# Graph attention on one core: behind each group of scores the projection runs before the transposes of x

## The chip, the cores and the metric

The kernel runs on one core of a Trainium2 chip. The metric is the device time of one execution in microseconds; the runs shown are given by their median. Five engines work side by side and wait for each other only through semaphores: TensorE (PE, with its weight loads as PEld), VectorE (DVE), ScalarE (ACT), GpSimd (POOL) and SyncE (SP), which issues the transfers.

## The reference, cut to what matters

```
x [32, 256, 384], adj [32, 256, 256]; 12 heads of 32 columns
q, k, v = x @ Wq + bq, x @ Wk + bk, x @ Wv + bv          (split into heads)
scores  = q @ k.T / sqrt(32) + beta * adj                 (-9e15 where adj <= 0)
probs   = softmax(scores)
out     = layernorm(x + probs @ v)                        (eps 1e-5)
```

## The kernel before, in words

A block is one of the B = 32 graphs. It has T = 2 tiles of 128 rows, C = 3 chunks of 128 input columns, G = 3 groups of J = 4 heads, so H = 12 heads. While block n goes through its heads h = 0 to 11, projections of block n + 1, transposes of block n + 2 and the values of block n - 2 are worked on in between.

TensorE's work outside the scores is cut into jobs, named by kind, part and block. Each writes one of four PSUM banks (`j_bank`), by its place in the ring modulo 4, and waits until the job four places earlier has been taken out of its bank (`wait_taken`).

- X(c, n): two transposes of chunk c of x (`turn_x`, L396). ACT copies the result to `xt_high` (L538), and DVE then subtracts that from the bank to make `xt_low` (L616). DVE's part waits for ACT's.
- K(g, n), Q(g, n), V(t, n): projections of nine matmuls (`project`, L387 for K and Q, L384 for V), taken by ACT alone (L534, L536).
- O(g, n): probabilities times values (`values`, L416), taken by ACT (L544). G(g, n): the result turned back (`turn_heads`, L424), taken by DVE (L623).
- T(h, n): four transposes of one head's probabilities (`turn`, L433), taken by ACT (L530) in the blocks up to the last. Only heads 10 and 11 go this way; the first ten are transposed by DVE in 32 x 32 pieces (`turn_blocks`, L635), and shuffled by DMA.

After the jobs of heads 0, 4 and 8 TensorE runs the sixteen score matmuls of the next group of four heads (`scores`, L463) into four `s_bank`s, each head in its own. Head 8 is followed by group 0 of block n + 1. Before them it waits until DVE has taken every maximum of the group before (`max_ready`).

DVE takes two maxima per head from `s_bank` (`maxima`, L600), which also write `neg_scores`. ACT follows with the two exponentials (`exps`, L518). ACT's order in head h is `exps` of head h + 2 and then the jobs of h in the order of the table. DVE's order in heads 1 and 5 is the maxima of heads h + 3 and h + 4 and then X; in head 9 X stands between the two (heads 12 and 13 there are heads 0 and 1 of the next block). Behind X come G, the maxima of head h + 4 at h = 2, 6 and 10, and in block n's head 10 one `turn_blocks`, then, in head 11, the maxima of head 15 (head 3 of the next block).

The order of everything is written out by hand in `jobs_of`: TensorE's program, ACT's and DVE's are all made from that one table, and so is the ring of banks. The change touches the table of the middle blocks, n = 1 to 30 (L81 to L95). Block n + 2 exists up to n = 29, so 29 blocks have X jobs by this table.

Of the kernel before, what the change touches and what calls it, by code (L numbers as in the profile page):

```python
# [34 lines left out]
def graph_attention_program(nc, x, adj, wq, bq, wk, bk, wv, bv, beta, out):  # L35
# [22 lines left out]
    def by_blocks(n, h):  # L58
        return h < block_heads(n)
# [5 lines left out]
    def jobs_of(n, h):  # L65
        if n == 0:

            jobs = {
                0: (("K", 2, 0),),
                1: (("K", 0, 1),),  # L70
                2: (("Q", 0, 1),),
                3: (("K", 1, 1),),
                4: (("V", 0, 0),),
                5: (("Q", 1, 1),),
                6: (("V", 1, 0), ("Q", 2, 1)),
                7: (("V", 0, 1),),
                9: (("X", 0, 2), ("K", 2, 1)),
                10: (("X", 1, 2),),
                11: (("X", 2, 2), ("V", 1, 1)),
            }  # L80
        elif n < B - 1:  # L81
            jobs = {
                0: (("O", 0, n - 2),),
                1: (("X", 0, n + 2), ("K", 0, n + 1)),
                2: (("G", 0, n - 2), ("Q", 0, n + 1)),
                3: (("K", 1, n + 1),),
                4: (("O", 1, n - 2),),
                5: (("X", 1, n + 2), ("Q", 1, n + 1)),
                6: (("G", 1, n - 2), ("Q", 2, n + 1)),
                7: (("V", 0, n + 1),),  # L90
                8: (("O", 2, n - 2),),
                9: (("X", 2, n + 2), ("K", 2, n + 1)),
                10: (("G", 2, n - 2),),
                11: (("V", 1, n + 1),),
            }  # L95
        else:
            jobs = {
                0: (("O", 0, n - 2),),
                1: (("O", 1, n - 2),),
                2: (("G", 0, n - 2), ("O", 2, n - 2)),  # L100
                3: (("G", 1, n - 2),),
                4: (("G", 2, n - 2),),
                5: (("O", 0, n),),
                7: (("G", 0, n), ("O", 0, n - 1)),
                8: (("O", 1, n - 1),),
                9: (("G", 0, n - 1), ("O", 2, n - 1), ("G", 1, n - 1), ("O", 1, n)),
                10: (("G", 2, n - 1), ("G", 1, n)),
            }
        turn = () if by_blocks(n, h) else (("T", h, n),)
        return turn + tuple(job for job in jobs.get(h, ()) if 0 <= job[2] < B)  # L110
# [4 lines left out]
    second_jobs = (("K", 1, 0),) + tuple(("X", c, 1) for c in range(C))  # L115
    last_jobs = (("O", 2, B - 1), ("G", 2, B - 1))
    ring = [*first_jobs, *second_jobs, *(job for n in range(B) for h in range(H) for job in jobs_of(n, h)), *last_jobs]
    place = {job: r for r, job in enumerate(ring)}

# [33 lines left out]
    with ctx:  # L153
# [216 lines left out]
        def _(pe):  # L370
# [124 lines left out]
            for n in range(B):  # L495
                for h in range(H):
                    jobs = jobs_of(n, h)
                    if not by_blocks(n, h):
                        run(jobs[0])
                        jobs = jobs[1:]  # L500
                    for job in jobs:
                        run(job)
                    if h % J == 0:
                        if h < H - J:
                            scores(n, h // J + 1)
                        elif n + 1 < B:
                            scores(n + 1, 0)
# [4 lines left out]
        def _(act):  # L512
# [58 lines left out]
            for n in range(B):  # L571
                for h in range(H):
                    s = H * n + h
                    if s + 2 < B * H:
                        exps(s + 2)
                    for job in jobs_of(n, h):
                        take(job)
# [388 lines left out]
```

## Time and profile before

| | us |
|---|---|
| median of 3 runs (lowest, highest) | 622.64 (622.37, 623.55) |
| profiled execution | 621.97 |
| its span | 620.1 |
| PE busy | 601.8 |
| DVE busy | 582.7 |
| ACT busy | 574.8 |
| POOL busy | 492.6 |

The span is the time from the first to the last instruction on the core; 1.87 us of the execution lie around it. Busy times are unions of the instructions' spans. Matmuls overlap in the array, so the distance from one group's first weight load to the next group's tells more of TensorE than the busy time does.

### The profile page before, as it was taken

The numbers are of one execution on the slowest core, as the hardware profiler recorded it, in microseconds if no ns is written. First come the engines' busy times: TensorE is split into PE (matmuls) and PEld (weight loads), VectorE is DVE, ScalarE is ACT, GpSimd is POOL, SyncE is SP. The second block draws the span as 40 slices with busy tenths as digits, with TensorE's granted clock in tenths as the row PEclk, the third lists the DMA queues.
The fourth block names the chain that finished last, engine by engine and source line by source line (L and its number), as shares of the span: only waits on it lengthen the run. The fifth ranks groups of instructions, "written<-read, shape, count | busy, mean of one in ns | idle before, by whom it ended". The sixth has DMA issues, their size and how long they took to land. (4 is left out here: it accounts for less than half of the span.)

```text
span 620.1 us, 20691 instructions
## 1 busy us (share of the span) xinstructions
PE 601.8 (97%) x6080; PEld 488.2 (79%) x6080; DVE 582.7 (94%) x2235; ACT 574.8 (93%) x2063; POOL 492.6 (79%) x669
## 2 busy tenths in 40 slices
PE   8999999999999999999999999999999999999991
PEld 7887878787888878787878788888878787878760
DVE  4989999999999999999999999999999999999786
ACT  4999999999999999999999999999999999999981
POOL 1334448988888888888898888898888889889793
PEclk9999999999999999999999999999999999999996
DMA  6258879988888988888998888898888898887832
GB/s 202 80 120 193 180 169 220 203 193 203 200 201 198 236 177 202 201 203 195 220 199 196 203 201 199 202 222 185 203 202 200 197 227 187 201 201 176 198 92 101
DMA packets 56190, 117.61 MB, mean 190 GB/s; under 512 B 10512, under 2 KB 12304, under 8 KB 56080
## 3 DMA queue, kind: packets, MB, share of 16 engines
q1 hardware_dynamic: 54992, 116.10, 80.6%
q8 instruction: 50, 0.82, 0.6%
q14 instruction: 60, 0.49, 0.3%
q10 hardware_dynamic: 1088, 0.20, 0.2%
HBM read 22.94 MB, written 12.58 MB: 57 GB/s over the span
## 5 line engine op out<-in xcount | busy, mean ns | idle before, releaser
L518 ACT ACTIVATE probs<-neg_scores,neg_max 128x256 f32<-128x256 f32 x768 | 382.5, 504 | 1.8 <-DVE neg_max L600 1.3
L600 DVE CUSTOM_DVE_ANT_0 neg_scores<-s_bank,bias_sb 128x256 f32<-128x256 f32 x768 | 280.1, 414 | 16.3 <-PE s_bank L463 15.1
L635 DVE STREAM_TRANSPOSE blocks<-probs 128x512 f32<-128x512 f32 x308 | 196.8, 685 | 0.3 <-ACT probs L518 0.3
L518 ACT ACTIVATION_READ_ACCUMULATOR probs<-neg_scores,neg_max 128x1 f32 x768 | 150.9, 197 | 0.0
L463 PE MATMUL s_bank<-qk 32*128 32x256 f32 x1536 | 110.0, 400 | 1.0 <-ACT qk L534 0.6
L387 PE MATMUL j_bank<-xt_high,w_high 128*128 128x256 f32 x567 | 110.1, 302 | 0.3 <-ACT qk L534 0.3
L534 ACT ACTIVATE qk<-j_bank,qk_bias 128x256 f32<-128x256 f32 x192 | 89.9, 469 | 21.0 <-PE j_bank L387 17.6
L463 PEld LDWEIGHTS s_bank<-qk 32*128 32x128 f32 x1536 | 69.5, 184 | 41.0 <-ACT qk L534 13.1
L898 POOL TENSOR_SCALAR att<-att,rstd,shift 128x384 f32<-128x384 f32 x58 | 95.7, 1656 | 6.3 <-POOL shift L895 6.3
L416 PE MATMUL j_bank<-shuffled,v_sb 128*32 128x256 f32 x1232 | 98.1, 385 | 0.2 <-ACT blocks L530 0.2
L387 PE MATMUL j_bank<-xt_high,w_low 128*128 128x256 f32 x567 | 97.0, 279 | 0.0
L387 PE MATMUL j_bank<-xt_low,w_high 128*128 128x256 f32 x567 | 96.9, 279 | 0.0
L862 POOL TENSOR_TENSOR att<-att,x_sb 128x768 f32<-128x768 f32 x30 | 55.5, 1850 | 39.2 <-DVE att L623 38.4
L387 PEld LDWEIGHTS j_bank<-xt_high,w_high 128*128 128x128 f32 x567 | 79.4, 189 | 2.3 <-issue 1.8
L387 PEld LDWEIGHTS j_bank<-xt_low,w_high 128*128 128x128 f32 x567 | 79.7, 188 | 0.0
L387 PEld LDWEIGHTS j_bank<-xt_high,w_low 128*128 128x128 f32 x567 | 79.6, 188 | 0.0
L843 POOL TENSOR_SCALAR bias_sb<-adj_sb 128x512 f32<-128x512 f32 x30 | 59.9, 1998 | 22.4 <-DMA adj_sb<-in_adj_dram 16.7
L846 POOL TENSOR_SCALAR adj_sb<-adj_sb,beta_col 128x512 f32<-128x512 f32 x31 | 62.1, 2004 | 13.3 <-DVE bias_sb L648 10.2
L856 POOL TENSOR_TENSOR x_sb<-x_sb,bv_row 128x768 f32<-128x768 f32 x32 | 59.1, 1848 | 8.2 <-DMA bv_row<-in_L_gnn_bv_dram 7.9
L416 PEld LDWEIGHTS j_bank<-shuffled,v_sb 128*32 128x32 f32 x1232 | 37.2, 109 | 35.2 <-issue 15.1
L600 DVE DVE_READ_ACCUMULATOR2_ANT neg_max<- 128x1 f32 x768 | 63.9, 83 | 0.0
L888 POOL TENSOR_SCALAR nt_b<-var_eps,rstd 128x1 f32<-128x1 f32 x174 | 58.3, 347 | 6.5 <-POOL rstd L881 6.2
(81 smaller groups left out, 918.4 us busy)
## 6 DMA issues: line engine op xcount, KB each, us to landing
shuffled<-blocks SPq DMA_DIRECT2D x480, 160.0 KB, 4.2
x_sb<-in_x_dram SPq DMA_DIRECT2D x32, 384.0 KB, 6.1
out_dram<-att SPq DMA_DIRECT2D x30, 384.0 KB, 4.0
adj_sb<-in_adj_dram SPq DMA_DIRECT2D x32, 256.0 KB, 6.2
shuffled<-blocks SPq DMA_DIRECT2D x16, 128.0 KB, 2.5
blocks<-in_L_gnn_Wq_dram SPq DMA_DIRECT2D x1, 576.0 KB, 5.7
blocks<-in_L_gnn_Wk_dram SPq DMA_DIRECT2D x1, 576.0 KB, 8.0
blocks<-in_L_gnn_Wv_dram SPq DMA_DIRECT2D x1, 576.0 KB, 5.0
```

What stands on the lines that cost most here:

```text
L387: mm = pe.matmul(b[:, 0:N], wp[:, q, c, a * P:(a + 1) * P], xp[:, n % 2, c, :], start=(m == 0), stop=(m == 3 * C - 1))
L416: mm = pe.matmul(b[HD * j:HD * (j + 1), 0:N], v_sb[:, n % 4, k, h * HD:(h + 1) * HD], probs_k, start=(k == 0), stop=(k == T - 1))
L463: mm = pe.matmul(s_bank[j][:, t * N:(t + 1) * N], qk[rows, n % 2, 0, g, t * P:(t + 1) * P], qk[rows, n % 2, 1, g, :], start=True, stop=True)
L518: nc.scalar.activation(probs[:, (T * s + t) % (T * NX), :], neg_scores[:, (T * s + t) % (T * NH), :], ACT.Exp, bias=neg_max[:, n % 2, t, h ...
L534: ins = nc.scalar.activation(qk[:, n % 2, q, a, :], b[:, 0:N], ACT.Identity, bias=qk_bias[:, q, a:a + 1])
L600: nc.vector.tensor_tensor_reduce(neg_scores[:, (T * s + t) % (T * NH), :], s_bank[h % J][:, t * N:(t + 1) * N], bias_sb[:, n % 2, t, :], - ...
L635: nc.vector.transpose(blocks[:, n % 2, :, h, :, :].rearrange("p k t q -> p t k q"), probs[:, slot:slot + T, :].rearrange("p t (k q) -> p t ...
L843: nc.gpsimd.tensor_scalar(key_order(bias_sb[:, n % 2, :, :]), by_keys(adj_sb[:, :, :]), 0.0, MASKED, ALU.is_le, ALU.mult).then_inc(not_edg ...
L846: nc.gpsimd.tensor_scalar(adj_sb[:, :, :], adj_sb[:, :, :], 0.0, beta_col[:, 0:1], ALU.max, ALU.mult).then_inc(adj_beta_ready, 1)
L856: nc.gpsimd.tensor_tensor(x_sb[:, n % XB, :, :], x_sb[:, n % XB, :, :], bv_row[:, :].unsqueeze(1).to_broadcast([P, T, D]), ALU.add).then_i ...
L888: b_at[t] = link(nc.gpsimd.tensor_scalar(nt_b[:, t:t + 1], var_eps[:, t:t + 1], rstd[:, t:t + 1], rstd[:, t:t + 1], ALU.mult, ALU.mult))
L898: nc.gpsimd.tensor_scalar(att[:, n % 3, t, :], att[:, n % 3, t, :], rstd[:, t:t + 1], shift[:, t:t + 1], ALU.mult, ALU.subtract).then_inc( ...
```

## The change

In the middle blocks the projection that stands in the same head as an X job is put ahead of it, at heads 1, 5 and 9. No job is added or taken away.

```diff
         elif n < B - 1:
             jobs = {
                 0: (("O", 0, n - 2),),
-                1: (("X", 0, n + 2), ("K", 0, n + 1)),
+                1: (("K", 0, n + 1), ("X", 0, n + 2)),
                 2: (("G", 0, n - 2), ("Q", 0, n + 1)),
                 3: (("K", 1, n + 1),),
                 4: (("O", 1, n - 2),),
-                5: (("X", 1, n + 2), ("Q", 1, n + 1)),
+                5: (("Q", 1, n + 1), ("X", 1, n + 2)),
                 6: (("G", 1, n - 2), ("Q", 2, n + 1)),
                 7: (("V", 0, n + 1),),
                 8: (("O", 2, n - 2),),
-                9: (("X", 2, n + 2), ("K", 2, n + 1)),
+                9: (("K", 2, n + 1), ("X", 2, n + 2)),
                 10: (("G", 2, n - 2),),
                 11: (("V", 1, n + 1),),
             }
```

## Rows read from the trace of the kernel before

**Rows 1.** Page, part 1: busy time, share of the span, instructions of each engine.
```profile
PE 601.8 (97%) x6080; PEld 488.2 (79%) x6080; DVE 582.7 (94%) x2235; ACT 574.8 (93%) x2063; POOL 492.6 (79%) x669
```
**Rows 2.** Windows: busy time of each engine, PE clock, DMA share, GB/s.
```profile
core 0: us, PE busy (x) PEld busy (x) DVE busy (x) ACT busy (x) POOL busy (x), PEclk, DMA share, GB/s
41.50:580.00 538.50, 538.09 (x5493) 437.57 (x5495) 523.47 (x2022) 518.19 (x1883) 452.13 (x601) 1.00 0.88 200
250.26:268.61 18.35, 18.35 (x193) 14.91 (x190) 18.14 (x71) 17.64 (x66) 16.31 (x23) 1.00 0.87 201
```
**Rows 3.** Waits: who waited for whom; us in total, times, longest.
```profile
ACT qk L534 <- PE j_bank L387: 17.6, 44, 0.5
DVE neg_scores L600 <- PE s_bank L463: 15.1, 32, 1.6
```
**Rows 4.** Timeline of weight loads, one block: start, us, ..., [idle before <- releaser].
```profile
250.26 0.74 PEld L463 LDWEIGHTS s_bank<-qk 32*128 32x128 f32 x16 [0.41 <-ACT v_sb L536]
251.33 0.20 PEld L396 LDWEIGHTS j_bank<-ident,x_sb 128*128 128x128 f32 x2 [0.33 <-ACT heads_t L544]
251.50 0.42 PEld L387 LDWEIGHTS j_bank<-xt_high,w_high 128*128 128x128 f32 x3
...
252.57 0.46 PEld L433 LDWEIGHTS j_bank<-ident,probs 128*128 128x128 f32 x4
253.00 0.25 PEld L424 LDWEIGHTS j_bank<-ident,heads_t 128*128 128x128 f32 x2
253.22 0.47 PEld L433 LDWEIGHTS j_bank<-ident,probs 128*128 128x128 f32 x4
253.66 0.48 PEld L384 LDWEIGHTS j_bank<-w_high,xt_high 128*128 128x128 f32 x3
...
256.43 0.74 PEld L463 LDWEIGHTS s_bank<-qk 32*128 32x128 f32 x16 [0.41 <-ACT probs_t L530]
...
262.28 0.74 PEld L463 LDWEIGHTS s_bank<-qk 32*128 32x128 f32 x16 [0.41 <-ACT qk L534]
...
268.60 0.74 PEld L463 LDWEIGHTS s_bank<-qk 32*128 32x128 f32 x16 [0.41 <-ACT v_sb L536]
```
**Rows 5.** Timeline of weight loads in block 30, which has no X job.
```profile
575.27 0.41 PEld L387 LDWEIGHTS j_bank<-xt_high,w_high 128*128 128x128 f32 x3 [0.33 <-issue]
...
576.33 0.24 PEld L424 LDWEIGHTS j_bank<-ident,heads_t 128*128 128x128 f32 x2
576.54 0.42 PEld L387 LDWEIGHTS j_bank<-xt_high,w_high 128*128 128x128 f32 x3
```
**Rows 6.** Timeline of ACT around head 9 of the same block as Rows 4.
```profile
251.99 0.36 ACT L538 ACTIVATE xt_high<-j_bank 128x256 fp32r<-128x256 f32 x1
252.88 0.47 ACT L534 ACTIVATE qk<-j_bank,qk_bias 128x256 f32<-128x256 f32 x1 [0.52 <-PE j_bank L387]
253.25 0.50 ACT L518 ACTIVATE probs<-neg_scores,neg_max 128x256 f32<-128x256 f32 x1
```
**Rows 7.** Timeline of DVE from head 9 on, the same block.
```profile
252.39 0.42 DVE L616 TENSOR_TENSOR xt_low<-j_bank,xt_high 128x256 fp32r<-128x256 f32 x1
252.73 0.41 DVE L600 CUSTOM_DVE_ANT_0 neg_scores<-s_bank,bias_sb 128x256 f32<-128x256 f32 x1
...
253.53 0.42 DVE L623 TENSOR_TENSOR att<-j_bank,inv_sum 128x256 f32<-128x256 f32 x1
...
255.84 0.08 DVE L600 DVE_READ_ACCUMULATOR2_ANT neg_max<- 128x1 f32 x1
...
261.29 0.09 DVE L600 DVE_READ_ACCUMULATOR2_ANT neg_max<- 128x1 f32 x1
...
269.95 0.42 DVE L600 CUSTOM_DVE_ANT_0 neg_scores<-s_bank,bias_sb 128x256 f32<-128x256 f32 x1 [0.37 <-PE s_bank L463]
```
**Rows 8.** Timeline in block 0, where scores came right behind DVE's maxima.
```profile
24.62 0.08 DVE L600 DVE_READ_ACCUMULATOR2_ANT neg_max<- 128x1 f32 x1
...
24.82 0.77 PEld L463 LDWEIGHTS s_bank<-qk 32*128 32x128 f32 x16 [0.37 <-issue]
...
25.93 0.19 PEld L387 LDWEIGHTS j_bank<-xt_high,w_high 128*128 128x128 f32 x1 [0.33 <-issue]
```

## The prediction

> **What bounds the kernel now.** I read the page's first part, then the windows, the waits, and one block's timelines side by side. Part 1 shows TensorE busy for 97% of the span, DVE for 94% and ACT for 93% [rows 1], so TensorE leads but two others are close. The windows say it more sharply: over the 538.5 us of the middle TensorE is busy for 538.09 at a granted clock of 1.00, and in one block of 18.35 us it is busy throughout, DVE for 18.14 and ACT for 17.64 [rows 2]. TensorE sets the pace. DVE has 0.2 us of slack by that, a little more by its waits: its one regular wait is for the scores, 0.47 us a block (15.1 us in 32 times), and ACT's is for the projections, 17.6 us in 44 times [rows 3]. In the block that I follow, the scores start at 250.26, 256.43, 262.28 and 268.60 [rows 4]: legs of 6.17 (from group 0's scores in head 8 to the next), 5.85 and 6.32, together 18.34.
>
> What the reader should look at is how near DVE's release of the scores comes. The scores at 256.43 need all maxima of the group before, and the last of these ends at 255.84 + 0.08 = 255.92 [rows 7]. Those at 262.28 have theirs at 261.29 + 0.09 = 261.38. How long TensorE takes from such a release is seen in block 0: maximum over at 24.70, first weight load at 24.82, so 0.12 us [rows 8]. The first slack is thus 256.43 - 256.04 = 0.39 us, the second 262.28 - 261.50 = 0.78 us. A delay on DVE of more than 0.39 us between heads 9 and 0 stops TensorE.
>
> **The change part by part.** No instruction is added or removed. There are 3 places in each of 29 blocks (n = 1 to 29), 87 in all, and no DMA moves; SP's and POOL's programs are the same. All three engines' orders change, because all come from the table.
>
> *TensorE's own time.* Before, scores, X, K, next: X's loads start 1.07 after those of the scores, of which 0.33 is idle (the full-width load waits behind the row-packed scores), X takes 251.50 - 251.33 = 0.17 and K 252.57 - 251.50 = 1.07 [rows 4]. Block 30 shows K right behind the scores: the same 0.33 idle, and 576.33 - 575.27 = 1.06 [rows 5]. So K gains 0.01, and the idle stays. No row shows X behind K, but G is the same kind of job (two f32 transposes of 128x128): behind K and ahead of K it takes 576.54 - 576.33 = 0.21 [rows 5], between two T jobs 253.22 - 253.00 = 0.22 [rows 4]. X then costs 0.21, and the G or T behind it, which now follows a transpose and not a projection, 0.01 more. The sum at a place is -0.17 + 0.21 + 0.01 - 0.01 = +0.04. Its bounds: X behind K could be as cheap as now (0.17, which with K's gain makes -0.01) and as dear as 0.22, with 0.01 behind it (+0.05). I take 0.04, since G is nearest. Were that all, 87 x 0.04 = 3.5 us.
>
> The Trainium skill would have it otherwise (TensorE: Matmul & The Clock Gate, "Back-to-back issue gap"): it gives N/2.4 + 2.5 ns from one warm matmul to the next, 56 ns at N = 128. By it X behind K would cost 0.11 us and each place would gain 0.06. The trace has 0.11 per transpose wherever f32 transposes follow one another (T's four take 253.66 - 253.22 = 0.44 [rows 4]), twice the page's figure, so I keep the row's and put the page's result among the rivals.
>
> *ACT, in order.* Before, ACT takes X at 251.99 while K still runs, then idles 0.52 until K is released at 252.88 [rows 6]: X's copy is hidden in that gap. Now K comes first. K's result is there 0.17 + 0.01 earlier, at 252.70; ACT has been free since 251.99 and waits 0.71 for it. K's copy holds ACT for 0.37 (252.88 to 253.25), so X's copy starts at 253.07 and ends 0.36 later, at 253.43. Before, it ended at 252.35. Queued behind are the exponentials, which start some 0.1 us later than before; nobody waits for them that soon.
>
> *DVE, in order.* `xt_low` started 0.04 behind the end of ACT's copy (252.35 to 252.39 [rows 7]); now it starts at 253.47, **1.08 us later**. In head 9 the maxima of one head only stand ahead of it, so DVE stalls, and queued behind it are the maxima of the next head, G, two more heads' maxima and one block transpose. One pause behind it goes: the two maxima from 252.73 would be over at 253.42, G came at 253.53, so 0.11 was a wait for G. The last maximum of the group is then over at 255.92 + 1.08 - 0.11 = 256.89, and 0.12 later the scores load: 257.01 and not 256.43. **That is 0.58 us in this leg**, in which TensorE's own 0.04 is contained. Scores that had to wait fill an emptied array: 25.93 - 24.82 = 1.11 against 251.33 - 250.26 = 1.07, so 0.03 more [rows 4, 8]. Bounds for both together: 0.46 with no release time and no refilling, 0.71 with a further 0.1 us for handovers that the rows don't show.
>
> *Heads 1 and 5.* Both heads' maxima stand ahead of X there, 0.69 us more cover. `xt_low` can't start before the scores' start + 3.21 (253.47 - 250.26). DVE now arrives at about that moment, as it has run 0.97 us later since head 9; its stall is under 0.1 us. The maxima that release the scores of head 4 are over at 261.38 + 0.97 + 0.06 = 262.41, plus 0.12 is 262.53, and TensorE is there at 262.28 + 0.58 + 0.03 + 0.04 = 262.93. So TensorE leads these legs: +0.04 each. Back at head 8 the first maximum waits for the scores again (1.35 us behind their start: 268.60 to 269.95), and DVE arrives at that time within 0.1 us, so the lateness doesn't add up from block to block.
>
> *Banks.* T(11), four places behind K, needs K's copy (252.70 + 0.47 + 0.12 = 253.29) and is due at 253.26; that is nothing. The job four places behind X is now V(1) in head 11; it needs `xt_low`, over at 253.47 + 0.42, and the release of 0.12 makes 254.01. V stood at 253.66, with the place's own 0.04 at 253.70. It waits 0.31, and V and O lead to the scores 2.77 later (256.43 - 253.66), at 256.78. That is ahead of 257.01, so it lies beneath DVE's release; if that release were not there, this wait would cost 0.35 in its place.
>
> *Sum.* 0.58 + 0.03 + 2 x 0.04 = 0.69 us a block, a period of 19.04. Times 29 it is 20.0 us. On the profiled execution, 620.1 + 1.87 around it = 621.97, it gives 642.0; the median is 0.67 above that execution, so 642.7.
>
> **The rivals.**
> *Only TensorE's order counts.* If the maxima reach their release with DVE's stall inside the slack, 3.5 us remain: 626. For it: TensorE is the engine that is always busy, and the slack of 0.39 is real. Against it: the stall less the pause is 0.97, and the bank wait lies behind it.
> *The bank wait alone.* If the release is cheaper than I read it and V's wait decides, the leg costs 0.35, the block 0.43 and the whole 12.5 us: 635.
> *All three legs stall.* If handovers cost 0.2 more than the rows say in each leg, and the 0.4 us of slack at heads 1 and 5 is used up, the block costs 1.0 to 1.1: 621.97 + 29 x 1.05 + 0.67 = 653.
> *Not slower.* X behind K is fully overlapped: it costs 0.11, the place gains 0.06, 87 places gain 5.2 us, and the DVE stall is absorbed: 617. It decides once X behind K costs less than 0.18. For it speaks that the transposes' first load now runs beneath K's last matmul; against it, G in just that position takes 0.21. With X at 0.17 to 0.18 this case lands within 1 us of before.
> *The change doesn't do what it says.* The order is taken from the table by all engines, and the 29 blocks with X lie under it. I see no way for it to stay without effect, and give it nothing of its own.
>
> **How the numbers follow.** The forecast (638 to 648) has 0.62, the bank wait or a partly hidden stall (630 to 638) 0.15, TensorE's order alone (624 to 628) 0.08, all legs 0.09, not slower 0.06. A change of under 0.2% (1.2 us) can't be told from none here. The last case splits into 0.03 faster and 0.03 the same, all others are slower: 0.94. The range from 630 to 650 holds 0.8 of this. It takes in the bounds of the first leg, which give 638 (29 x 0.54) and 646 (29 x 0.79) on the median.
>
> **What would show it.** Right: in the windows a period near 19.0; in the waits a new line of the scores (L463) waiting for DVE's neg_max, once a block, about 0.5 us; ACT's wait for the projection at L534 up from 0.52 to about 0.7 in head 9; `xt_low` (L616) waiting for `xt_high` some 1.0 us in head 9 and hardly in heads 1 and 5; DVE's wait for the scores nearly gone; X's loads 0.21 apart from the next job's. Wrong: scores with no wait for DVE, then the time is 626 or less; waits at all three groups' scores, then it is 650 or more. The step that I trust least is the handover chain K, ACT, ACT, DVE, maxima, scores, since each link was read from one place.

## The result and the profile after

The changed kernel takes 642.79 us (median of 4 executions) against 622.50 before. The ratio is 1.0325, 95% interval 1.0311 to 1.0340: 3.3% slower. One of the four executions was disturbed (2480 us) and is left out of the ratio; the other three lie between 642.30 and 643.17, with a median of 642.41, which is 19.9 us above before. The forecast was 642.7, in a range of 630 to 650.

The profiled execution took 643.17 us, with a span of 641.4. Part 1 of its page, which answers to [rows 1], and two windows, which answer to [rows 2] (the middle, and one block from group 0's scores to the next group 0's):

```profile
PE 613.2 (96%) x6080; PEld 494.2 (77%) x6080; DVE 582.9 (91%) x2235; ACT 582.6 (91%) x2063; POOL 491.8 (77%) x669
```
```profile
41.50:580.00 538.50, 530.12 (x5300) 427.86 (x5299) 504.08 (x1948) 506.97 (x1816) 432.88 (x576) 1.00 0.83 193
259.15:278.24 19.09, 18.82 (x193) 15.15 (x189) 17.92 (x70) 17.94 (x65) 16.31 (x23) 1.00 0.78 195
```

The counts of instructions are those of before. TensorE, which had 0.4 us of idle time in these 538.5 us, now has 8.4, and the block went from 18.35 to 19.09 us. Busy time of DVE and ACT per block hardly moved (18.14 to 17.92, 17.64 to 17.94), so no engine does more; they wait more. The granted clock is 1.00 in both windows, so it isn't the clock.

The waits of the changed kernel, beside [rows 3]:

```profile
...
DVE xt_low L616 <- ACT xt_high L538: 40.2, 36, 6.1
PEld s_bank L463 <- ACT v_sb L536: 31.2, 57, 0.8
ACT qk L534 <- PE j_bank L387: 31.0, 61, 1.7
...
PE s_bank L463 <- DVE neg_max L600: 7.7, 31, 0.4
...
DVE neg_scores L600 <- PE s_bank L463: 5.8, 6, 1.4
...
PE j_bank L387 <- DVE w_low L744: 1.3, 1, 1.3
```

Two of these lines stood so before:

```profile
PEld s_bank L463 <- ACT v_sb L536: 11.9, 29, 0.4
...
DVE xt_low L616 <- ACT xt_high L538: 7.9, 5, 6.2
```

The line that grew most is DVE waiting for `xt_high`, from 7.9 us in 5 times to 40.2 in 36. The line that costs is a small one further down, and hardly there before (0.2 us, once): the scores waiting for DVE's maxima, once a block. It shows 7.7 us, 0.25 a time, and not 17 (29 x 0.58), for two reasons. The same wait of the scores is also on their weight loads, where it is put down to ACT: their idle time there went from 0.41 to 0.69 in the rows below, 0.28 more. And another 0.27 of the block has gone by already, in V(1)'s wait for its bank: the idle time of 0.24 at 262.87, where V(1) comes 0.71 behind T(11) and not 0.44. With TensorE's own 0.05 this makes the 0.60 by which the leg is longer. The last line is in the start and not in the blocks: a projection of block 0 waited 1.3 us for weights, which the change doesn't touch.

The timeline of weight loads in that block, which answers to [rows 4] (columns: start, us, what, [idle before <- releaser]):

```profile
259.15 0.74 PEld L463 LDWEIGHTS s_bank<-qk 32*128 32x128 f32 x16 [0.41 <-ACT v_sb L536]
260.23 0.42 PEld L387 LDWEIGHTS j_bank<-xt_high,w_high 128*128 128x128 f32 x3 [0.33 <-ACT heads_t L544]
...
261.30 0.24 PEld L396 LDWEIGHTS j_bank<-ident,x_sb 128*128 128x128 f32 x2
261.51 0.47 PEld L433 LDWEIGHTS j_bank<-ident,probs 128*128 128x128 f32 x4
261.94 0.25 PEld L424 LDWEIGHTS j_bank<-ident,heads_t 128*128 128x128 f32 x2
262.16 0.47 PEld L433 LDWEIGHTS j_bank<-ident,probs 128*128 128x128 f32 x4
262.87 0.47 PEld L384 LDWEIGHTS j_bank<-w_high,xt_high 128*128 128x128 f32 x3 [0.24 <-issue]
...
264.63 0.59 PEld L416 LDWEIGHTS j_bank<-shuffled,v_sb 128*32 128x32 f32 x16 [0.25 <-issue]
265.91 0.77 PEld L463 LDWEIGHTS s_bank<-qk 32*128 32x128 f32 x16 [0.69 <-ACT v_sb L536]
...
271.83 0.74 PEld L463 LDWEIGHTS s_bank<-qk 32*128 32x128 f32 x16 [0.41 <-ACT qk L534]
...
278.24 0.31 PEld L463 LDWEIGHTS s_bank<-qk 32*128 32x128 f32 x8 [0.41 <-ACT v_sb L536]
```

ACT and DVE beside it, answering to [rows 6] and [rows 7]:

```profile
261.60 0.47 ACT L534 ACTIVATE qk<-j_bank,qk_bias 128x256 f32<-128x256 f32 x1 [0.49 <-PE j_bank L387]
261.97 0.38 ACT L538 ACTIVATE xt_high<-j_bank 128x256 fp32r<-128x256 f32 x1
```
```profile
262.38 0.42 DVE L616 TENSOR_TENSOR xt_low<-j_bank,xt_high 128x256 fp32r<-128x256 f32 x1 [1.10 <-ACT xt_high L538]
...
263.40 0.42 DVE L623 TENSOR_TENSOR att<-j_bank,inv_sum 128x256 f32<-128x256 f32 x1
...
265.72 0.08 DVE L600 DVE_READ_ACCUMULATOR2_ANT neg_max<- 128x1 f32 x1
```

And TensorE's two transposes of X, before and changed; their ends are modelled:

```profile
251.33 0.44 PE L396 MATMUL j_bank<-ident,x_sb 128*128 128x128 f32 x2
```
```profile
261.40 0.38 PE L396 MATMUL j_bank<-ident,x_sb 128*128 128x128 f32 x2
```

Read from 259.15 on. K's copy starts 2.45 behind the scores' start, X's copy 2.82, `xt_low` 3.23 with 1.10 of idle DVE ahead of it, the last maximum is over at 6.65 (265.80), and 0.11 later the next scores load, at 6.76. Before, that leg was 6.17 [rows 4]. The other two are 5.92 and 6.41 against 5.85 and 6.32.

The last two rows tell where X's lateness arises. Before, the transposes ended 1.51 behind the scores' start (251.77) and ACT, which was still busy, copied them at 1.73. Changed, they end at 2.63 (261.78) and ACT, which is copying K, takes them at 2.82. So of the 1.09 by which X's copy starts later, nearly all is already there when TensorE hands X over. The queue behind K's copy adds at most 0.15 (2.82 less 2.63 and a handover of 0.04, the distance from K's modelled end at 261.56 to its copy at 261.60).

### The profile page after: what moved, and what is told of

Read it like the earlier page. It is cut to its first block and busy times, and to the rows that moved or that the text cites. A ratio compares the mean times of both kernels' runs of the same rounds, so it can differ in the third digit from the quotient of the medians.

```text
span 641.4 us, 20691 instructions
## 1 busy us (share of the span) xinstructions
PE 613.2 (96%) x6080; PEld 494.2 (77%) x6080; DVE 582.9 (91%) x2235; ACT 582.6 (91%) x2063; POOL 491.8 (77%) x669
## 5 line engine op out<-in xcount | busy, mean ns | idle before, releaser
L387 PE MATMUL j_bank<-xt_high,w_high 128*128 128x256 f32 x567 | 112.7, 307 | 0.0
L463 PEld LDWEIGHTS s_bank<-qk 32*128 32x128 f32 x1536 | 70.9, 184 | 48.8 <-ACT v_sb L536 31.2
L616 DVE TENSOR_TENSOR xt_low<-j_bank,xt_high 128x256 fp32r<-128x256 f32 x96 | 40.3, 424 | 40.2 <-ACT xt_high L538 40.2
```

The source lines that it names most:

```text
L387: mm = pe.matmul(b[:, 0:N], wp[:, q, c, a * P:(a + 1) * P], xp[:, n % 2, c, :], start=(m == 0), stop=(m == 3 * C - 1))
L463: mm = pe.matmul(s_bank[j][:, t * N:(t + 1) * N], qk[rows, n % 2, 0, g, t * P:(t + 1) * P], qk[rows, n % 2, 1, g, :], start=True, stop=True)
```

## The experiments

Ratios are to the kernel before on the same chip, with their 95% interval. Legs (scores' first weight load to the next group's) are means over blocks 3 to 28, worked out from the timelines of weight loads; the leg of heads 9 to 0 is called the first, then those of heads 1 to 4 and 5 to 8. Before they are 6.17, 5.84 and 6.34; changed, 6.77, 5.89 and 6.40.

**Head 9 alone**

```diff
-                9: (("X", 2, n + 2), ("K", 2, n + 1)),
+                9: (("K", 2, n + 1), ("X", 2, n + 2)),
```

> K ahead of X in head 9 alone, heads 1 and 5 as before. Theory A (the handover chain K, ACT's two copies, xt_low, maxima, scores is paid in head 9 alone): the leg from group 0's scores to group 1's goes from 6.17 to about 6.76 us, with 0.03 for scores into an emptied array; 29 x 0.61 = 17.7, so about 640 us; the other two legs stay at 5.85 and 6.32. Rival B (each of the three places costs the same third of the 20 us): about 629. Rival C (only TensorE's order counts, 0.04 a place): 624.

Measured: 642.75 us, ratio 1.0325 (1.0311 to 1.0339): the whole loss, not 640. Legs 6.75, 5.96, 6.36. The first leg is as expected, so head 9 holds the cause and rivals B and C are out. The second was expected unchanged and is 0.12 longer, and that is where the 640 fell short. Weight loads and DVE there:

```profile
324.57 0.42 PEld L387 LDWEIGHTS j_bank<-xt_high,w_high 128*128 128x128 f32 x3
...
325.71 0.41 PEld L387 LDWEIGHTS j_bank<-xt_high,w_high 128*128 128x128 f32 x3
```
```profile
325.22 0.42 DVE L616 TENSOR_TENSOR xt_low<-j_bank,xt_high 128x256 fp32r<-128x256 f32 x1
```

Q(0) takes 1.14 to K(1) where it took 1.06: with X ahead of K in head 1, K(1) is the job four places behind X, and it starts 0.07 behind the end of `xt_low` (325.64). DVE, late since head 9, holds the bank. In the full change X is one place later there and the wait is gone; instead TensorE pays its 0.05. The two about balance, which is why one swap costs as much as three.

**Heads 1 and 5 alone**

```diff
-                1: (("X", 0, n + 2), ("K", 0, n + 1)),
+                1: (("K", 0, n + 1), ("X", 0, n + 2)),
...
-                5: (("X", 1, n + 2), ("Q", 1, n + 1)),
+                5: (("Q", 1, n + 1), ("X", 1, n + 2)),
```

> K or Q ahead of X in heads 1 and 5, head 9 as before. Theory A: xt_low waits some 0.4 us in head 1 and 0.1 in head 5, but the maxima that release the next scores stay ahead of TensorE by about 0.4 us and more, so only TensorE's own 0.04 a place shows: 58 x 0.04 = 2.3, about 625 us. Rival B (a third a place): about 636. The scores wait for no maximum.

Measured: 623.49 us, ratio 1.0016 (1.0007 to 1.0025). Legs 6.17, 5.82, 6.40. Two of the three swaps cost 1.0 us together. DVE does wait for `xt_high`: 0.32 in head 1 (0.4 was expected), nothing in head 5 (0.1 expected), and 0.13 in head 9, where X still stands ahead of K. Nothing comes of it: the scores' weight loads idle for 0.4 us a time as before, and from block 3 on no maximum releases them.

```profile
PEld s_bank L463 <- issue: 13.2, 33, 0.5
...
PEld s_bank L463 <- ACT probs_t L530: 12.2, 30, 0.4
PEld s_bank L463 <- ACT v_sb L536: 11.9, 29, 0.4
```

It is less than the 2.3 expected, since the second leg became shorter, by 0.02, while the third is longer by 0.06; more on that under the last experiment.

**The changed kernel, DVE takes X behind both heads' maxima**

```diff
-                        if h != 2 * J + 1 and s + 4 < B * H:
+                        if s + 4 < B * H:
                             maxima(s + 4)
                         for job in jobs_of(n, h):
                             take(job)
-                        if h == 2 * J + 1 and s + 4 < B * H:
-                            maxima(s + 4)
```

> The changed kernel, but DVE takes X in head 9 behind both heads' maxima, as it does in heads 1 and 5. xt_low still can't start before the scores' start + 3.2 us. Theory A with the bank wait: DVE's release of the scores comes 0.7 us earlier and no longer decides; what is left is V(1)'s wait for the bank that xt_low holds, about 0.27 us, so the block costs 0.31 + 0.04 + 0.08 = 0.43 and the whole about 635 us; TensorE's wait for neg_max before the scores is gone, V(1) waits. Rival D (the bank wait costs nothing): 626. Rival E (what counts is that xt_low comes late at all, whatever is queued behind it): 643 as the changed kernel.

Measured: 634.66 us, ratio 1.0203 (1.0189 to 1.0217). Legs 6.51, 5.89, 6.40. TensorE's and ACT's orders are those of the changed kernel and `xt_low` starts at the same time behind the scores (3.23), but 8 of the 20 us are gone. So the changed kernel's loss hangs on what stands behind `xt_low` on DVE, and rival E is out. What is left in the first leg is the bank: V(1) loads 0.08 behind the end of `xt_low` (316.39 + 0.42).

```profile
316.18 0.47 PEld L433 LDWEIGHTS j_bank<-ident,probs 128*128 128x128 f32 x4
316.89 0.47 PEld L384 LDWEIGHTS j_bank<-w_high,xt_high 128*128 128x128 f32 x3 [0.24 <-issue]
...
319.67 0.74 PEld L463 LDWEIGHTS s_bank<-qk 32*128 32x128 f32 x16 [0.41 <-ACT v_sb L536]
```
```profile
316.39 0.42 DVE L616 TENSOR_TENSOR xt_low<-j_bank,xt_high 128x256 fp32r<-128x256 f32 x1 [0.42 <-ACT xt_high L538]
```

The four transposes of T take 0.44 and V comes after 0.71: a wait of 0.27. The scores' idle time is 0.41 again. Rival D is out as well.

**TensorE's order of before, ACT copies K first**

```diff
+    def swapped_pair(n, h):
+        return 1 <= n < B - 2 and h in (1, 5, 9)
+
+    def act_jobs(n, h):
+        jobs = jobs_of(n, h)
+        return jobs[::-1] if swapped_pair(n, h) else jobs
...
+                act_taken[r + 1], act_taken[r + 2] = act_taken[r + 2], act_taken[r + 1]
...
-                    for job in jobs_of(n, h):
+                    for job in act_jobs(n, h):
                         take(job)
```

The last added line makes the counts of `taken_a` that stand for the two jobs change places with them.

> TensorE's order as before (X, then K), but ACT copies K ahead of X in heads 1, 5 and 9, as in the changed kernel. Theory A (the cost is in ACT's order and what is behind it, not in TensorE's): slower than the changed kernel itself. xt_low starts at the scores' start + 3.39, and X's bank is now four places ahead of T(11), V(0) and K(1), which come 0.17 to 0.4 us sooner than the job four places behind X does there: waits of about 0.97 us in head 11, 0.35 in head 3 and 0.35 in head 7, a block 1.67 us longer, about 671 us (650 to 680). Rival C (the cost is TensorE's order): 622.5, as before.

Measured: 665.32 us, ratio 1.0692 (1.0677 to 1.0706). Legs 7.08, 6.14, 6.65: longer by 0.91, 0.30 and 0.31, against 0.97, 0.35 and 0.35 expected. TensorE runs exactly its old order, the kernel is twice as far behind as the changed one, and rival C is out: an order of ACT alone makes X late and costs. `xt_low` starts 3.40 behind the scores, 3.39 expected, though X's transposes are as early as before. But this isn't the road of the changed kernel. There X is late because TensorE turns it later, as the rows above show, and its loss is DVE's release of the scores; here the loss is the wait for X's bank, and the release isn't reached. How much of the changed kernel's loss would stay if ACT copied X ahead of K there was not run. By the rows `xt_low` would start at most 0.15 us earlier (an estimate), so most of it should stay. The wait in head 11:

```profile
309.37 0.25 PEld L437 LDWEIGHTS j_bank<-ident,heads_t 128*128 128x128 f32 x2
310.52 0.42 PEld L446 LDWEIGHTS j_bank<-ident,probs 128*128 128x128 f32 x4 [0.90 <-ACT xt_high L551]
```

(Lines are 13 further down in this kernel.) `xt_low` ran from 310.02 to 310.44, and T(11) took over its bank 0.08 later; the releaser that the line names, ACT's copy of X, was over by then.

**The third X behind V(1) in head 11**

```diff
-                9: (("X", 2, n + 2), ("K", 2, n + 1)),
+                9: (("K", 2, n + 1),),
                 10: (("G", 2, n - 2),),
-                11: (("V", 1, n + 1),),
+                11: (("V", 1, n + 1), ("X", 2, n + 2)),
```

> The kernel before, but the third X goes from ahead of K in head 9 to behind V(1) in head 11: further behind K than in the changed kernel. Theory A (lateness of X costs only where DVE must stand and wait for it with the group's maxima behind it, or where a due job needs its bank): ACT copies X in head 11 behind V's copy, DVE takes it behind the maxima of head 15 and the moments, when it is there, and no job four places behind is due. TensorE pays its own 0.04 to 0.05 in that leg and the release stays as it was: 624 us, block 18.40. Rival F (any X behind the projection costs what the changed kernel showed, or more the later it comes): 640 or more.

Measured: 623.84 us, ratio 1.0026 (1.0015 to 1.0037). Legs 6.24, 5.85, 6.32. `xt_low` comes about 3.5 us later than in the changed kernel (6.7 behind the scores of head 8, not 3.23) and the swap costs 1.6 us in place of 20. Rival F is out and lateness as such is free; 0.07 in the first leg is TensorE's own.

**The kernel before, DVE's order alone.** The diff is that of the third experiment, on the kernel before.

> The kernel before with DVE's order alone changed: in head 9 X behind both heads' maxima. A control for e3. xt_low starts some 0.6 us later without anybody's wait being added: its bank is needed by T(11) 0.8 us behind xt_low's old start plus its 0.42, so T(11) may wait: xt_low would end at 253.50, with 0.12 to release 253.62 against 253.22, a wait of up to 0.4 us; the maxima come no later. Theory A: the bank wait costs 0.4 x 29 = 11.6, 634 us. If banks cost nothing: 622.5.

Measured: 629.22 us, ratio 1.0113 (1.0099 to 1.0127). Legs 6.41, 5.85, 6.32. The wait is where it was expected, but 0.25 and not 0.4: the end of `xt_low` had been put at 3.24 behind the scores and is at 3.15, and its handover at 0.12 where it is 0.07. So DVE's order of before, with X between the maxima, is there for the bank; neither order of DVE suits a late X.

**Projections of Q and K ahead of the values**

```diff
-                6: (("G", 1, n - 2), ("Q", 2, n + 1)),
-                7: (("V", 0, n + 1),),
+                6: (("G", 1, n - 2), ("V", 0, n + 1)),
+                7: (("Q", 2, n + 1),),
```

> An attempt to beat the kernel before, on TensorE's own time. Q(2) and V(0) change places, so that head 8's values follow a projection of Q and not one of V. Before, V then O costs 1.77 where V then a transpose costs 1.51 (0.26 more), K then O 1.265 where K then V costs 1.057 (0.21 more); V then K costs some 0.02 on the way. Expected: 0.03 us a block, 621.7 us, near what can be told. The same if the distance between the matmuls of a projection falls into the other of its two values (114 or 118 ns), which can move a block by 0.05 either way.

Measured: 622.77 us, ratio 1.0007 (0.9997 to 1.0017): no difference. From G(1) to the values it is 3.03 to 3.05 where before it was 3.03 to 3.07: Q(2) behind V(0) takes 1.32 to the values and not 1.265, which uses up the gain.

> e7, and K(2) and V(1) change places too, in heads 9 and 11: V stands behind X, K ahead of O. On TensorE the sum of the starts from X to O goes from 4.10 to about 4.05; with e7's 0.03 it is 0.08 a block: 620.3 us. Against it: V is 0.45 us longer than K, so ACT waits longer in head 9 (0.5 becomes 1.0) where it has 0.7 us of slack a block; should its copies come late for the banks or its exponentials for DVE's block transposes, the result is 625 or more.

Measured: 629.45 us, ratio 1.0113 (1.0098 to 1.0129), no gain but a loss. Legs 6.30, 5.97, 6.35. TensorE's own order is no shorter: from X to O(0) it is 4.10 as before and not 4.05, since T(10) behind V takes 0.50 to G and not 0.43. And TensorE waits. With V in head 9 the job G behind it comes later, DVE waits 0.29 for `xt_high` and 0.26 for G, and the last maximum (314.86 + 0.08) releases the scores at 315.06, after 0.12. The first leg is bound by the same release as in the changed kernel, by another road. The second is 0.12 longer for the same reason as in the first experiment: Q(0) takes 1.14 to K(1), whose bank X's late `xt_low` holds.

**Head 1 alone**

```diff
-                1: (("X", 0, n + 2), ("K", 0, n + 1)),
+                1: (("K", 0, n + 1), ("X", 0, n + 2)),
```

> K ahead of X in head 1 alone. In the run with heads 1 and 5 swapped the leg of head 1 took 5.82 us against 5.84 before, since K(1) and Q(0) behind the swap ran with 114 ns between matmuls and not 118. If that belongs to the order in this leg, the leg is again 5.82, the other two are as before and the whole is 29 x 0.02 = 0.6 us faster, 621.7. If it was chance, the leg is 5.89 (0.05 more) and the whole 1.4 us slower, 623.7.

Measured: 625.30 us, ratio 1.0047 (1.0034 to 1.0060), above both forecasts. Legs 6.18, 5.88, 6.40. The short leg didn't belong to the order: here the second leg has the 0.04 that the rows of before had promised. The third is 0.06 longer though its order is untouched, and neither forecast had that. DVE waits for `xt_high` in head 1, here 0.32 us, and is late in head 5, where X still stands ahead of Q(1): V(0)'s place in the ring is four behind X's, and Q(2) takes 1.10 to 1.18 to V(0) and not 1.06. V(0) starts 0.07 behind the end of `xt_low`, so that is the bank wait of the first experiment once more. No version here beats the kernel before.

## Why the prediction was right

*The first leg* was the whole of it, as forecast. The chain of handovers came out link by link: K's copy 2.44 behind the scores (measured 2.45), X's copy 2.81 (2.82), `xt_low` 3.21 (3.23), the last maximum 6.63 (6.65), the scores 6.75 (6.76). Its weight lies in what stands behind what, and not in any one duration: X's transposes move behind the whole of K, 1.08 later on TensorE (loads 2.15 behind the scores and not 1.07), and `xt_low` stalls DVE with the group's maxima behind it. The release time of 0.12, read from block 0 [rows 8], was 0.11 to 0.12 wherever the scores waited for DVE. The prediction told ACT's part as the reason why X's copy is late; the rows give that queue at most 0.15 of the 1.09. This doesn't touch the sum, which added up K's end and the two copies in order. The experiments show the ends of the chain: head 9 alone loses everything, the maxima moved out from behind `xt_low` give back 8 of the 20 us, and an X later still, with nothing due behind it, costs 1.6. The 12 us that remain in the third experiment are V(1)'s bank wait and TensorE's own order.

*A sign that failed.* ACT's wait for K in head 9 was to go from 0.52 to about 0.7. It is 0.49. The prediction had ACT free from 1.73 behind the scores, when X's copy used to start; in the changed kernel its exponentials run until 1.96 (261.11) and K's copy starts at 2.45. The forecast didn't need it, as K's end comes later than either.

*TensorE's own order* was put at 0.04 a place. In the changed kernel X takes 0.21 behind K (261.51 - 261.30), and K, X and T in heads 9 and 10 together 1.72 against 1.67 before, so 0.05. Head 1's place costs 0.05 by the same reckoning. In head 5 it is 0.08 or 0.01, by which of two rhythms before is taken (last section). The Trainium skill (TensorE: Matmul & The Clock Gate, "Back-to-back issue gap") has 56 ns at N = 128, from which the prediction made a gain, for an isolated matmul only. For a stream of weight loads and matmuls the same section of the Trainium skill gives about 81 ns; by that X would take 0.16 and the place would come out about even (an estimate). Neither is what the trace has: the two weight loads of X stand 0.10 to 0.11 apart behind K as well, and the measurement decides.

*Heads 1 and 5* cost nothing beyond TensorE's own, 0.04 and 0.06: the slack ahead of the scores swallowed DVE's wait, as the second experiment shows alone.

*The bank wait* of V(1) was forecast as 0.31, hidden beneath the release, and is 0.27. It stays hidden, and the third experiment uncovers it.

*The sum* was 20.0 us. The medians are 20.3 apart, or 19.9 with the 642.41 of the result's section. The profiled executions are 21.2 apart and their spans 21.3; 1.3 of that is there before block 1's first scores (32.73 against 31.43), ahead of every swapped pair, and `w_low` above was waited for in that part. The rest is 20.0. That it fits so closely is in part luck: the forecast knew nothing of the rhythms below, which can move the whole by 2 us either way, and two swaps measured by themselves cost 1.0 us where 2.3 was expected. What I had not counted is the coupling that the first and the last experiment show: where X keeps its old place behind a late DVE, its bank holds up the projection four places behind it by 0.04 to 0.12. In the full change it has no place to act.

## What to carry to other kernels

An order of issue is the order of every in-order engine behind it. Before moving a short job behind a long one, look at how much later the short job's result is ready, and at what is queued behind its last taker; here a job of 0.2 us went behind one of 1.07, and DVE stood still for 1.1 us with the maxima behind it. The engine that is busy for 97% still hangs on a release with 0.4 us of slack, and such slacks (release to first use, per group) are read from the timeline, not from busy shares. And a job's place in a ring of four banks says which later job pays for its lateness: move it by one and another job pays.

## What the runs showed of the hardware that was not expected

The nine matmuls of a K or Q projection run in one of two rhythms, 117 to 118 ns or 113 to 114 ns apart, with nothing waiting. In the changed kernel Q(0) in head 2 takes 1.05 to K(1) in one block and 1.02 in the next, in turn, and K(1) 1.26 or 1.22 to the values. In other kernels the rhythm holds for many blocks at the same place and then changes over: in the kernel before, K in head 9 took 1.07 up to block 20 and 1.04 from block 21 on, and Q in head 5 the reverse. The third leg went from 6.32 to 6.39 with it, so that the mean of 6.34 given above is of both. In block 21 one Q(0) took 1.14 to K(1) and not 1.06; whether that set off the change is not shown. With heads 1 and 5 swapped, head 1's leg had the fast rhythm in all blocks from 3 on (-0.07 us a block), with head 1 alone in one block only. What sets it is open. It can move a kernel of this kind by about 2 us (29 x 0.07, an estimate), against the 3.5 at which TensorE's own cost of this change was put.

Handovers measured on the way: DVE's `xt_low` to the next user of the bank on TensorE 0.07 to 0.08 us, DVE's maximum to the scores 0.11 to 0.12.
